# Expert stage of a convolution, router and expert kernel: written out, with four buffers each way

## The reference

```python
y = jnp.fft.irfft(u_f * k_f, n=n)[..., :Lq]
y = y + u_m * D[:, None]
...
logits = x @ gate_w.T
probs = jax.nn.softmax(logits.astype(jnp.float32), axis=-1)
vals, idx = jax.lax.top_k(probs, TOP_K)
vals = vals / jnp.sum(vals, axis=-1, keepdims=True)
...
h = jax.nn.silu(gate_out) * up_out
d_r = d.reshape(H, NUM_EXPERTS, INTER)
out = jnp.einsum('bei,hei,be->bh', h, d_r, w)
```

## Time and profile before

| | before |
|---|---|
| median of 3 runs | 540.82 us (539.96 to 542.36) |
| the profiled execution | 542.34 us |
| its span | 540.5 us |
| PE busy | 457.0 us (85%) |
| DVE, ACT, POOL busy | 204.6, 99.1, 172.1 us |
| moved by DMA | 119.94 MB, mean 222 GB/s |

### The profile page before, as it was taken

How to read it: one execution, slowest core, us unless ns; L and a number is a source line. 1 busy time by engine, 2 the same in 40 slices (tenths; PEclk the granted TensorE clock), 3 DMA queues, 4 the chain that set the end, 5 groups by cost and what they waited for, 6 DMA issues and landing times.

```text
span 540.5 us, 9417 instructions
## 1 busy us (share of the span) xinstructions
PE 457.0 (85%) x2867; PEld 391.3 (72%) x2868; DVE 204.6 (38%) x560; ACT 99.1 (18%) x230; POOL 172.1 (32%) x215
## 2 busy tenths in 40 slices
PE   0479799999998998958899889899899798899881
PEld 0469798988888988857777667677677576677660
DVE  6914334533334325494233233232333223333321
ACT  3930000000000000200122122221222122222210
POOL 5244222233221100063144332353343334344331
PEclk9989899999999999968899999999999989999996
DMA  8958978788888889922278878989887968868553
GB/s 297 312 159 274 310 244 274 274 266 279 285 289 256 290 269 333 333 106 77 75 216 215 213 182 247 249 232 258 231 180 225 274 185 183 241 134 176 83 80 69
DMA packets 39466, 119.94 MB, mean 222 GB/s; under 512 B 7442, under 2 KB 15890, under 8 KB 39314
## 3 DMA queue, kind: packets, MB, share of 16 engines
q1 hardware_dynamic: 18418, 73.49, 41.4%
q0 software_dynamic: 11808, 37.76, 31.6%
q10 hardware_dynamic: 9216, 8.39, 4.6%
HBM read 94.68 MB, written 38.57 MB: 247 GB/s over the span
## 4 chain that ended last, share of the span: by engine, by line
PE 44%; DMA 35%; issue 8%; DVE 8%; POOL 2%; ACT 0%; POOLq 0%; ACTq 0%; DVEq 0%; SPq 0%
PE conv_ps L988 18%; DMA out<-od,to_row 12%; PE conv_ps L1097 11%; DMA ys<-y_rows,from_row 10%; DMA arena<-k_rows 7%; PE conv_ps L1115 7%; DMA k_rows<-k_sb 6%; PE turn_ps L1105 4%; PE conv_ps L1083 1%; PE turn_ps L999 1%; DVE tmp L637 1%; POOL out L458 1%; DVE od L933 1%; POOL arena L430 1%; DVE mask_t L786 1%
## 5 line engine op out<-in xcount | busy, mean ns | idle before, releaser
L988 PE MATMUL conv_ps<-arena 128*128 128x256 f32 (+7 forms) x1024 | 158.4, 311 | 16.5 <-DMA arena<-k_rows 9.6
L988 PEld LDWEIGHTS conv_ps<-arena 128*128 128x128 f32 x1024 | 150.3, 194 | 24.6 <-issue 13.5
L1097 PE MATMUL conv_ps<-w_gu,ys_t 128*128 x656 | 135.9, 361 | 13.8 <-issue 11.5
L1097 PEld LDWEIGHTS conv_ps<-w_gu,ys_t 128*128 128x128 f32 x656 | 122.3, 192 | 33.3 <-issue 32.9
L458 POOL DMA_INDIRECT out<-od,to_row x40 | 63.5, 1587 | 132.3 <-DMA out<-od,to_row 70.1
L1115 PE MATMUL conv_ps<-w_d,hid_t 112*128 x160 | 76.9, 603 | 0.0
L742 DVE TENSOR_TENSOR arena<-conv_ps,mask_t 128x256 f32<-128x256 f32 x64 | 26.9, 423 | 97.9 <-PE conv_ps L988 96.8
L442 POOL DMA_INDIRECT ys<-y_rows,from_row x42 | 44.5, 1059 | 46.4 <-PE turn_ps L1105 34.3
L933 DVE TENSOR_SCALAR od<-conv_ps,weight_now 128x512 f32<-128x512 f32 x40 | 30.0, 751 | 72.2 <-DMA out<-od,to_row 47.1
L1105 PE MATMUL turn_ps<-ident,ys 128*128 128x128 f32 x336 | 45.8, 281 | 13.3 <-DMA ys<-y_rows,from_row 13.3
L1105 PEld LDWEIGHTS turn_ps<-ident,ys 128*128 128x128 f32 x336 | 39.7, 144 | 18.5 <-DMA ys<-y_rows,from_row 17.0
(11 more groups left out here) (151 smaller groups left out, 309.8 us busy)
## 6 DMA issues: line engine op xcount, KB each, us to landing
arena<-k_rows SPq DMA_DIRECT2D x14, 2048.0 KB, 10.9
w_gu<-gu_t SPq DMA_DIRECT2D x16, 896.0 KB
arena<-x_time SPq DMA_DIRECT2D x16, 512.0 KB, 4.0
y_rows<-y_blk ACTq DMA_DIRECT2D x64, 128.0 KB, 7.4
w_d<-d_t SPq DMA_DIRECT2D x16, 448.0 KB
arena<-k_rows SPq DMA_DIRECT2D x8, 512.0 KB, 6.0
ys<-y_rows,from_row POOLq DMA_INDIRECT x42
out<-od,to_row POOLq DMA_INDIRECT x40
```

The costliest lines, as they stand in the source:

```text
L988: last = nc.tensor.matmul(conv_ps[:, h, d * B:C * B], toep[:, p, h, d * P:(d + 1) * P], u_t[:, p, h, 0:(C - d) * B], start=(d == 0), stop= ...
L1097: last = nc.tensor.matmul(gu_ps, ys_t[:, p, c, :], w_gu[:, bass.ds(buf * (C * GU) + c * GU, GU)], start=(c == 0), stop=(c == C - 1))
```

## The change

MT is 47 and LEAST is 32, so USUAL is 40. PE, ACT, DVE and POOL now run 40 tiles as straight code with constant tile numbers; only then comes a condition (more than 40 tiles, then more than 44), which is false here. No tile 40 or 41 is touched any more. `ys` and `od` have four buffers (R = 4): gather(t) waits for turn(t-4), ACT and DVE wait for scatter(t-4) before they write od. POOL's order is scatter(t-1), gather(t+4). A scatter looks up three counts instead of one and waits for the three scatters before it: all landed where its tile begins another expert, otherwise the ones that they displaced (the first of them wait for all in any case). Empty slots have an index out of bounds in the scatter too; to_row and the spare rows' indices are gone, as is the copy of one weight per tile (`weight_of`, L926). TensorE looks up a tile's buffer and expert once, behind the turn of the tile, where it did so before gate_up and again before down.

Six experts are resident, in the arena: three are loaded where four were, the next two behind the last two copies of x, the sixth when the convolution is done. SP's later loads are for expert e+6 when expert e is through. POOL clears a quarter of ys at the start instead of all of it, and the other three buffers between the marks of `not_first` and the third group's factors.

```diff
-WB = 4
+R = 4
+WB = 6
+WE = C * GU + L
+USUAL = LEAST + E // 2
+SPANS = ((0, USUAL), (USUAL, USUAL + 4), (USUAL + 4, MT))
...
-        flat = sb("arena", [P, 2 * HG * L + H * 2 * LO + 2 * HG * C * B + 2 * C * P])
-        toep = flat[:, 0:2 * HG * L].rearrange("p (s h l) -> p s h l", s=2, h=HG)
-        at = 2 * HG * L
+        early = 3 * WE + WE - 512
+        flat = sb("arena", [P, early + H * 2 * LO + 2 * HG * C * B + 2 * C * P + 2 * HG * L])
...
+        od = flat[:, at:at + R * L].rearrange("p (s n) -> p s n", s=R)
...
-        def pairs(eng, used, pair):
-
-            pair(1)
-            with eng.Fori(1, (LEAST - 1) // 4 + 1) as i:
-                pair(2 * i)
-                pair(2 * i + 1)
-            with eng.Fori((LEAST - 1) // 2 + 1, (MT - 3) // 2) as i:
-                with eng.If(used >= 2 * i + 1):
-                    pair(i)
-
-        def first_step(s):
-
-            return min(s - (s + 1) % 2, MT - 2)
+        def spans(eng, tiles_of):
+
+
+            tiles_of(*SPANS[0])
+            used = tiles_in_use(eng)
+            for lo, hi in SPANS[1:]:
+                with eng.If(used >= lo + 1):
+                    tiles_of(lo, hi)
...
-            for e in range(WB):
+            for e in range(3):
                 load_expert(e)
             for q in range(6, 8):
                 copy_x(q)
+            sp.wait_ge(factors_made, G)
+            load_expert(3)
+            load_expert(4)
+            sp.wait_ge(conv_done, G * HG)
+            load_expert(5)
...
             def gather(t):
 
-                if t >= 2:
-                    pool.wait_ge(turned, t - 1)
+                if t >= R:
+                    pool.wait_ge(turned, t - R + 1)
                 nc.gpsimd.indirect_dma_start(
-                    out=ys[:, t % 2, :], out_offset=None, in_=y_rows,
+                    out=ys[:, t % R, :], out_offset=None, in_=y_rows,
                     in_offset=bass.IndirectOffsetOnAxis(ap=from_row[:, t:t + 1], axis=0),
-                    bounds_check=TOK - 1, oob_is_err=False).then_inc(gathered[t % 2], 16)
+                    bounds_check=TOK - 1, oob_is_err=False).then_inc(gathered[t % R], 16)
 
             def scatter(t):
 
 
-                if t >= 3:
-                    earlier = pool.value_load(waits_i[0:1, t:t + 1], min_val=16, max_val=16 * (MC // 2))
+                earlier = range(max(0, t - R + 1), t)
+                counts = [16 if s < R else pool.value_load(waits_i[0:1, t - s - 1, t:t + 1], min_val=16,
+                                                           max_val=16 * (MC // R)) for s in earlier]
                 pool.wait_ge(od_act, t + 1)
                 pool.wait_ge(od_dve, t + 1)
-                if t >= 3:
-                    pool.wait_ge(scattered[(t - 1) % 2], earlier)
-                elif t >= 1:
-                    pool.wait_ge(scattered[(t - 1) % 2], 16)
+                for s, count in zip(earlier, counts):
+                    pool.wait_ge(scattered[s % R], count)
                 nc.gpsimd.indirect_dma_start(
-                    out=out, out_offset=bass.IndirectOffsetOnAxis(ap=to_row[:, t:t + 1], axis=0),
-                    in_=od[:, t % 2, :], in_offset=None, compute_op=ALU.add,
-                    bounds_check=TOK + P - 1, oob_is_err=True).then_inc(scattered[t % 2], 16)
-
+                    out=out, out_offset=bass.IndirectOffsetOnAxis(ap=from_row[:, t:t + 1], axis=0),
+                    in_=od[:, t % R, :], in_offset=None, compute_op=ALU.add,
+                    bounds_check=TOK - 1, oob_is_err=False).then_inc(scattered[t % R], 16)
 
             pool.wait_ge(sources_made, 1)
             for p in range(2):
                 pool.wait_ge(y_stored[p], 64 * (G // 2))
-            gather(0)
-            gather(1)
-            gather(2)
-
-            pool.wait_ge(lists_made, 1)
+            pool.wait_ge(ys_cleared, 2)
+            for t in range(R):
+                gather(t)
+
             pool.wait_ge(x_copied, 8 * 16)
             pool.wait_ge(spare_out, 16)
-            pool.wait_ge(enters_made, 1)
-            used = tiles_in_use(pool)
-            for t in range(1, MT + 2):
-                if t + 2 < MT:
-
-                    if first_step(t + 1) <= LEAST:
-                        gather(t + 2)
-                    else:
-                        with pool.If(used >= first_step(t + 1)):
-                            gather(t + 2)
-                if t >= 2:
-
-                    if first_step(t - 1) <= LEAST:
-                        scatter(t - 2)
-                    else:
-                        with pool.If(used >= first_step(t - 1)):
-                            scatter(t - 2)
-
-            with pool.If(used >= MT - 2):
-                pool.wait_ge(scattered[0], 16 * ((MT + 1) // 2))
-                pool.wait_ge(scattered[1], 16 * (MT // 2))
-            for p in range(2):
-                pool.wait_ge(scattered[p], (used + 1) // 2 * 16)
+            pool.wait_ge(enters_made, R - 1)
+
+            def tiles_of(lo, hi):
+
+                if lo > 0:
+                    for t in range(lo, min(lo + R, hi)):
+                        gather(t)
+                for t in range(lo, hi):
+                    if t >= lo + 1:
+                        scatter(t - 1)
+                    if t + R < hi:
+                        gather(t + R)
+                scatter(hi - 1)
+                if hi > USUAL:
+                    for p in range(R):
+                        pool.wait_ge(scattered[p], 16 * ((hi - 1 - p) // R + 1))
+
+            spans(pool, tiles_of)
+            for p in range(R):
+                pool.wait_ge(scattered[p], 16 * ((USUAL - 1 - p) // R + 1))
...
-            def weigh_half(t, p, i, first):
...
+            def weigh_half(t):
 
                 act.wait_ge(down_done, t + 1)
-                act.wait_ge(weight_copied, t + 1)
-                if not first:
-                    act.wait_ge(scattered[p], 16 * i)
-                nc.scalar.mul(od[:, p, 0:L // 2], down_ps[:, 0, :], weight_now[:, p:p + 1]).then_inc(od_act, 1)
...
+                if t >= R:
+                    act.wait_ge(scattered[t % R], 16 * (t // R))
+                nc.scalar.mul(od[:, t % R, 0:L // 2], down_ps[:, 0, :], slot_weight[:, t:t + 1]).then_inc(od_act, 1)
...
-            ts(shift[:, :], table_ps[:, 0:MC], 0.0, spare[:, 0:1], ALU.is_equal, ALU.mult)
-            stt(named[:, :], table_ps[:, 0:MC], -1.0, shift[:, :], ALU.add, ALU.add)
-            link(nc.vector.tensor_copy(slot_weight[:, :], table_ps[:, MC:]))
-            nc.vector.tensor_copy(to_row[:, :], named[:, :]).then_inc(lists_made, 1)
+            nc.vector.tensor_copy(slot_weight[:, :], table_ps[:, MC:]).then_inc(lists_made, 1)
...
-                                           ALU.mult, ALU.add).then_inc(enters_made, 1)
-
-            def turn_rest(t, p, first):
+            for k in range(1, R):
+                vec.scalar_tensor_tensor(waits_i[:, k - 1, k:], enters[:, k:], 16.0, landed_at[:, 0:MC - k],
+                                         ALU.mult, ALU.add).then_inc(enters_made, 1)
...
+            bufs, needs = {}, {}
+
+            def look_up(t):
+
+                bufs[t] = pe.value_load(tile_i[0:1, 0, t:t + 1], min_val=0, max_val=WB - 1)
+                needs[t] = pe.value_load(tile_i[0:1, 1, t:t + 1], min_val=1, max_val=E)
+
...
+            def tiles_of(lo, hi):
+
+                turn(lo)
+                if lo == 0:
+                    pe.wait_ge(experts_made, 1)
+                look_up(lo)
+                for t in range(lo, hi):
+                    gate_up(t)
+                    if t + 1 < hi:
+                        turn(t + 1)
+                        look_up(t + 1)
+                    if t > lo:
+                        down(t - 1)
+                    turn_hidden(t)
+                down(hi - 1)
+
+            spans(pe, tiles_of)```

ACT's and DVE's helpers change in the same way (`turn_half`, `gate`; `turn_rest`, `hidden`, `hidden_turned`, `weigh_rest`), and they run the same order of steps as before, from a `tiles_of` of their own.

On PE, at the end of a pair in the conditional loop before. Names: turn_ps<-ident,ys is the turn, tile_i the look-up, conv_ps<-w_d,hid_t the down product; ISA rows are the sequencer's register work.

```order
L1105 MATMUL turn_ps<-ident,ys 128x128 x7
L1109 TENSOR_LOAD tile_i
L1109 ISA x2
L1115 ISA [waits od_dve,od_act,hid_read]
L1115 MATMUL conv_ps<-w_d,hid_t 128x512
L1115 ISA
L1115 MATMUL conv_ps<-w_d,hid_t 128x512
L1121 MATMUL conv_ps<-ident,hid 112x128 [waits hid_made]
L260 UNCONDITIONAL_BRANCH
L259 REGISTER_ALU
L259 COMPARE_AND_BRANCH
```

More of the change, by code:

```diff
@@ L570, in turn_half, with gate @@
                                ).then_inc(yst_act, 1)
-            def gate(t, p, first):
+            def gate(t):
                 act.wait_ge(gu_done, t + 1)
-                if not first:
+                if t >= 2:
                     act.wait_ge(hid_made, t - 1)
```

(48 more changed lines are left out.)

175 lines of the change are left out of this document (58 added, 117 removed).

## The result

| | before | changed |
|---|---|---|
| median of 4 runs | 540.39 us (539.64 to 542.36) | 522.5 us (519.86 to 526.14) |
| ratio | | 0.9668, 95% interval 0.9603 to 0.9733 |
| profiled execution, its span | 542.34, 540.5 us | 519.86, 518.0 us |
| start of the first and second gate_up | 258.02, 265.38 us | 252.95, 258.09 us |
| 38 steps, second to fortieth gate_up | 250.6 us | 241.2 us |

What follows compares the result with a forecast made beforehand. TensorE was taken to bound the expert stage, with DMA close behind. From 540.8 us, 29.1 for removed waits less a residue of 8, plus 6.1 of tail, gave 27.2 off: 513.6 us, own range 506 to 521, 0.8 range 501 to 534.

Steps and rivals of the forecast that it cites:

- What bounds the kernel: Expert stage: TensorE bounds, undisturbed step 5.83 us; 38 steps fall from 250.6 to 221.5 us, a ceiling of 29.1.
- No branches: 38 steps: branch issue time goes, some 1.2 us in every second later step; look-ups behind the turn cost nothing.
- Four buffers: Gathers and scatters: 14.1 us for POOL's scatter and the gather's landing; expert changes still hold TensorE 0 to 1.6 us.
- The residue: 38 steps: TensorE waits left at changes of expert behind full tiles, 0 to 14 us, taken as 8.
- Empty slots: Scatters: 896 of 5120 slots not stored, 0.5 us of DMA per tile; no term of its own.
- Six experts: Weight loads: two experts' loads leave the stage; 0 by itself, since TensorE never waited for weights.
- The start: Ahead of the second gate_up: memset changes and fewer DVE operations gain 0; the first gate_up stays slow at 5.19 us.
- The tail: From the fortieth gate_up to the end: 18.4 us instead of 24.5, 6.1 less.
- TensorE alone: Rival: scatters land faster, no change of expert delays a gather, residue 0; 503.3 us, chance 0.20.
- The chain of landings: Rival: left-out slots cost as much as stored, fifteen expert changes leave 23.4 us residue; 533.1 us, chance 0.24.
- Starving: Rival: fetching straight code starves TensorE, some 16 more packets at 9.2 us; 569 us, chance 0.05.
- The signs: Trace: gate_up starts 5.8 us apart nearly throughout, software queue down some 3.7 MB; wrong if POOL is repeatedly over 5 us late.

Runs made afterwards that it cites:

- best: ahead, with TensorE's look-ups placed before the tile's turn and the first four scatters waiting by looked-up counts: 498.20 us, ratio 0.9292 to before.
- straight_in_order: Only the change's straight code (two buffers each way, four experts resident, empty slots stored), gather(t+3) issued ahead of scatter(t-1): 539.4 us, ratio 1.0028 to before.
- ahead: The changed kernel, with POOL issuing gather(t+5) ahead of scatter(t-1) instead of gather(t+4) behind it: 505.88 us.
- scatter_two: The changed kernel with two buffers of od instead of four, four of ys kept, POOL's order unchanged: 522.32 us.
- again: The changed kernel without any edit, run and profiled a second time as the base of its group: 522.95 us, ratio 0.9617 to before.
- stored_ahead: ahead, with empty slots stored to the spare rows: 512.69 to 529.52 us in four runs.
- stored: The changed kernel with empty slots stored to the spare rows again: 535.91 us, ratio 0.9885 to before.
- private: The changed kernel, each slot adding to its own row of a scratch tensor, no waits among scatters, out holding x alone: 503.36 us.

## Why the prediction was right, and where it was off

*What bounds the kernel.* Right: TensorE with a step of 5.83 us as the floor. It measured 5.73 to 5.74, so the ceiling for the 38 steps is not 29.1 but 32.6 us (250.6 - 218.0, reached by best).

*No branches.* The forecast put this and the buffers in one sum and named 1.2 us in every second of the later steps as the branches' own. straight_in_order shows no gain from it with two buffers each way (250.3 us against 250.6). The issue time of the earlier trace rows is gone, 9.5 us, but as much stands elsewhere: 4.4 more of waits for gathers and 5.2 of issue. That the look-ups behind the turn cost nothing was wrong where the turn is late: 0.4 to 1.6 us each time.

*Four buffers.* This is the term that was mis-sized. The residue was put at 8 us of 0 to 14. Against the forecast's own floor of 221.5 us it is 19.7, against the measured one of 218.0 it is 23.2. The waits for gathers themselves are 10.8 us, not far from the 8. What the sum left out is what a late turn brings with it, put at nothing: 4.8 us of issue for the look-ups, and 7.6 us more of busy time than in best (225.6 against 218.0), 3.5 of them two down products at the 1.2 GHz level (3.56 and 3.67 us instead of 1.88).

The working saw the gather behind the scatter and counted 14.1 us for it, but for one change of expert at a time. And it took the order on POOL as given, where it had been turned round: with the old order, in ahead, 16.2 of the 23.2 us go, and the other 7.0 go with the two waits that best takes out. It also left out that the first scatters wait for each other whatever their expert, though the change's order shows it. What that costs is not shown by itself: in scatter_two the fourth scatter is free of it, and two steps there are together as long over 5.73 (8.2 us) as the two of the changed kernel (8.5). Of the two depths, ys is worth 19.3 us in the right order, od nothing in the wrong one; od in the right order was not tried.

*Empty slots.* It was right that they matter beyond the tail, and too high per tile: 0.3 us instead of 0.5. Taken out of the changed kernel alone they cost 13.0 us, of 17.9 that the whole change gained.

*Six experts.* 0 was forecast; 1.9 us was measured, inside the spread.

*The start.* The forecast had nothing here, which was wrong, and by luck on the side that made up for part of the residue. The second gate_up came 7.3 us earlier. Of these, the lists end 3.3 us earlier (from_row at 245.22 against 248.48), the first gather lands in 4.45 instead of 5.38 us, and the first turn and gate_up ran at the full clock (1.09 and 3.29 us instead of 1.97 and 5.19). The last is chance: in again, the same kernel, the first gate_up took 6.30 us, and the second came 4.6 us earlier than before. In eleven of the twelve experiments the first gate_up starts at 249.7 to 254.5 us, also in straight_in_order, whose time is that of before; in stored_ahead it starts at 260.5. So it is not shown that the change earns the earlier start. There is one profile of before, from the slowest of its runs, and why its convolution ended later stays open.

*The tail.* 18.7 us against 18.4 forecast. stored and straight_in_order keep 24.7 and 24.5, so the saving is the left-out slots, as the sum had it: the scatter with one row and the one with none.

```profile
505.85 1.55 POOL L459 DMA_INDIRECT out<-arena,from_row  x1 [3.31 <-DVE arena L904]
511.03 1.56 POOL L459 DMA_INDIRECT out<-arena,from_row  x1 [3.64 <-issue]
```

The one with a row was followed by the last 5.2 us later, where the two stood 6.9 apart before.

*The rivals.* TensorE alone gave 503.3 us on the condition that scatters land faster. ahead and private come to that time (505.9, 503.4), and best passes it with landings of 8.2 us: what it takes is that gathers do not wait behind scatters. The chain of landings was the right mechanism. Its residue, 19.7 us against the forecast's floor, lies between the forecast's 8 and the rival's 23.4, and not for the reason given, that left-out slots are as dear as stored ones; with the slots stored the time is 535.9, near the rival's 533.1. Starving did not happen. The instruction queues on the page of after:

```profile
q8 instruction: 23, 0.38, 0.3%
q14 instruction: 16, 0.13, 0.1%
```

They carry 39 packets where the forecast had 40, and no gap at even distances is left in best, busy for 160.00 of 160.00 us: fetching straight code was covered. By the Trainium skill, "Runtime: NRT & Kernel Launch", section "Instruction fetch mechanics", straight fetching runs ahead and is mostly hidden; the trace agrees.

*The signs.* 28 of the 38 steps are 5.7 to 5.8 us, which is most but not "nearly throughout". ACT and DVE no longer wait for a scatter ahead of od, and the software queue moved 4.2 MB less (33.57 against 37.76). But POOL behind by more than 5 us again and again was named as a sign against the forecast, and it is what the trace shows: its scatters waited 97.0 us for landings, 16 times, up to 8.5 us. The time was in the range; by this sign the mechanism was not the one forecast in full.

## What to carry to other kernels

When a queue carries both loads and stores, look at who stands behind whom before counting buffers: a gather whose buffer is free and whose transfer is needed must not be queued behind a store that waits for a landing. Here one swap in POOL's queue was worth nearly as much as the whole change (16.4 us against 17.9). In the wrong order four buffers of ys only made good what the order cost (806 to 522 us); in the right one they gained (525 to 506). And a stall that a profile shows in the bounding engine need not be worth its time: the branches' 9.5 us of issue went, and as much came back, in part as longer waits for gathers, in part as issue at the place to which the look-ups had been moved.

## What was not expected of the hardware

A slot left out of an indirect DMA by its bound still costs something: storing 896 of 5120 slots less took 0.3 us of 4.09 per tile off the DMA engines, and the small packets grew from 1619 to 2146 in a window of 160 us. A stall can cost TensorE twice: after 2.24 us without work, a turn and 1.62 us of issue the next product ran 3.56 us instead of 1.88, at the 1.2 GHz level; that happened behind two of the eight late turns. And DMA engines at a share of 0.84 are no obstacle in themselves: at the same share the kernel before waited for gathers, and best has TensorE busy without a gap.
